# Walking sixteen batches with a loop on the chip instead of straight-line code, in a gated window-attention and router kernel

## The chip, the cores and the metric

The kernel runs on one core of a Trainium2 chip. Its time is device microseconds from start to end of one execution on that core; lower is better. The core has a matrix engine (TensorE, PE in the profile), VectorE (DVE), ScalarE (ACT) and GpSimd (POOL), and a fifth queue, SyncE (SP), which here only issues DMAs. Each of the five has a sequencer of its own that reads its own list of instructions and meets the others only through semaphores.

## The reference

`x` and `ctx` are 16 batches of 256 channels by 2048 positions, float32.

```python
x = x + tanh(g_xattn) * xattn(layernorm(x), ctx)   # layernorm over the 2048 positions
x = x + tanh(g_ffn) * ffn(layernorm(x))

# xattn: 8 heads of 32 channels; position t sees the 16 keys t-8 .. t+7
q, k, v = Wq @ x + bq, Wk @ ctx + bk, Wv @ ctx + bv
attn = softmax(q . k_window * 32**-0.5)
out = Wo @ (attn . v_window) + bo

# ffn: each row of 2048 is routed over 64 experts, the best 8 of the softmax are kept
scores = softmax(flat @ router_weight.T + router_bias)
out = flat * sum(top8) + w_dense @ expert_bias
```

## The kernel before

A batch is cut into four chunks of 512 positions (`NCH`), and the unit of the program is a **step**: chunk `c` of batch `b`, with `par`, which of two buffers the batch uses. A step works on several chunks at once: the scores and softmax of its own chunk (four units, each a half chunk of a 128-channel group), attention and output projection of the chunk before (`attend`, `output`), router columns of the chunk two back (`rows`, `router`), queries of the next chunk, keys and values of the chunk two ahead, and in chunks 2 and 3 the router's result for the batch before (`mixture` on PE, `finish` on DVE).

The order inside a step is written out by hand, once for each engine. On PE it is: `attend(0)`, `queries(1)`, `rows(1)`, `scores(0)`, `attend(1)`, `router`, `scores(1)`, `scores(2)`, mixture, `output(0)` and `output(1)`, `scores(3)`, `values(0)` and `values(1)`, `queries(0)` of the next chunk, `rows(0)`, `keys(0)` and `keys(1)`. A scores unit is one mask matmul of 384 columns and 32 small ones on 32-row tiles; an attend is 51 matmuls of up to 64 columns; a projection (L1099) is 6 matmuls of 512 columns.

DVE takes maxima, shifts, sums and transposes the probabilities (`turn`, L882), and in between it runs three chains of very small operations, each of which waits for the one before by semaphore: the reciprocal roots of the two layer norms (L771 to L783, in chunks 3 and 0) and the router's top 8 (L1023 to L1075, in chunk 1). ACT evicts, takes exponentials and makes the high halves; POOL makes the low halves and the residual sums.

All ordering between operations goes through `need` (L288), a semaphore wait for a count. Semaphores are never set back, so the counts grow with the batch: `nth(b, c, off)` is 4b + c + off + 1, `done(UNITS, ...)` is 16b + something, and others go with 2b, 5b, 8b, 12b, 15b, 64b or 256b. Before the change Python knows every count, and each wait carries a constant. `need` leaves a wait out where the count is zero or less, and `live` and `seq` leave out work beyond the first and the last batch:

```python
        def walk(step):

            for n in range(-2, N + NCH):
                step(n // NCH, n % NCH, (n // NCH) % 2)
```

`N` is 64, so each engine's program is 70 steps of straight-line code with no jump in it.

Of the kernel before, what the change touches and what calls it, by code (L numbers as in the profile page):

```python
# [58 lines left out]
def gated_window_attention_and_router(nc, x, ctx, g_xattn, g_ffn, wqT, bq, wkT, bk, wvT, bv, woT, bo,  # L59
# [11 lines left out]
    with ExitStack() as stack:  # L71
# [200 lines left out]

        def live(b, c, off):

            return 0 <= NCH * b + c + off < N

        def final(b, g, j):

# [4 lines left out]
            return c >= 2 and seq(b - 1)  # L283

        def seq(b):
            return 0 <= b < B

        def need(eng, s, value):  # L288

            if value > 0:  # L290
                eng.wait_ge(s, value)

        def walk(step):

            for n in range(-2, N + NCH):
                step(n // NCH, n % NCH, (n // NCH) % 2)

        def place(c, off):

# [22 lines left out]
        @block.sync  # L322
        def _(sp):

            for i, w in enumerate((wkT, wvT)):
                sp.dma_start(wkv_raw[:, i], w.rearrange("(g p) o -> p g o", g=G)).then_inc(kv_ld, 16)
            for i, v in enumerate((bk, bv)):
                sp.dma_start(bias_kv[:, i], v).then_inc(kv_ld, 16)
            for ch in range(NCH):
                sp.dma_start(x1[0][:, :, cols(ch)],  # L330
                             ctx[0, :, cols(ch)].rearrange("(g p) t -> p g t", g=G)).then_inc(sq0_ld[ch], 16)
            sp.dma_start(wq_raw[:], wqT.rearrange("(g p) o -> p g o", g=G)).then_inc(w_ld, 16)
            sp.dma_start(att[:, :, 0:C], woT.rearrange("(g p) o -> p g o", g=G)).then_inc(w_ld, 16)
            sp.dma_start(bias_q[:], bq).then_inc(w_ld, 16)
            sp.dma_start(bias_o[:], bo).then_inc(w_ld, 16)
            sp.dma_start(gates[:, 0:1], g_xattn.partition_broadcast(P)).then_inc(w_ld, 16)
            sp.dma_start(gates[:, 1:2], g_ffn.partition_broadcast(P)).then_inc(w_ld, 16)
            sp.dma_start(c_in[:], ctx[0, :, cols(0)].rearrange("(g p) t -> p g t", g=G)).then_inc(ctx_in, 16)
            for ch in range(NCH):
                sp.dma_start(x_in[:, :, cols(ch)],  # L340
                             x[0, :, cols(ch)].rearrange("(g p) t -> p g t", g=G)).then_inc(x_ld[ch], 16)
            sp.dma_start(c_sq[:], ctx[1, :, cols(0)].rearrange("(g p) t -> p g t", g=G)).then_inc(sq_ld, 16)
            sp.dma_start(rb[:], rbias.partition_broadcast(P)).then_inc(r_ld, 16)
            sp.dma_start(wr[:], wrT.rearrange("(n p) e -> p n e", p=P)).then_inc(r_ld, 16)
            for half in range(2):
                sp.dma_start(x1[1][half * E:(half + 1) * E, 0, :], experts).then_inc(r_ld, 16)

            sp.wait_ge(sq_rdy, NCH + 1)
            sp.dma_start(c_sq[:], ctx[1, :, cols(1)].rearrange("(g p) t -> p g t", g=G)).then_inc(sq_ld, 16)

            def step(b, c, par):
                if live(b, c, 0):

                    turned, freed = nth(b, c, 0), nth(b, c, -1)
                    for g in range(G):
                        need(sp, vt_rdy[g], turned)
                        need(sp, av_mm[g], freed)
                        for h in range(HPG):
                            sp.dma_start(v_diag[head(h), g, :, head(h)],
                                         v_turn[head(h), g].rearrange("p (j d) -> p j d", d=SUB)).then_inc(vd_ld[g], 16)  # L360
                if live(b, c, 3) and live(b, c, 2):

                    ch, db = place(c, 3)
                    rows_in = ctx[b + db, :, cols(ch)].rearrange("(g p) t -> p g t", g=G)
                    need(sp, cl_rdy, nth(b, c, 2))
                    sp.dma_start(c_in[:], rows_in).then_inc(ctx_in, 16)
                if live(b, c, 8):

                    ch, db = place(c, 8)
                    rows_in = ctx[b + db, :, cols(ch)].rearrange("(g p) t -> p g t", g=G)  # L370
                    need(sp, sq_rdy, nth(b, c, 7))
                    sp.dma_start(c_sq[:], rows_in).then_inc(sq_ld, 16)
                if live(b, c, 0):

                    rows_in = x[b, :, cols(c)].rearrange("(g p) t -> p g t", g=G)
                    for g in range(G):
                        need(sp, x1_rdy[g], nth(b, c, -1))
                    sp.dma_start(x_res[:], rows_in).then_inc(res_in, 16)
                if live(b, c, 5) and live(b, c, 1):

                    ch, db = place(c, 5)
                    rows_in = x[b + db, :, cols(ch)].rearrange("(g p) t -> p g t", g=G)
                    need(sp, xl_rdy, nth(b, c, 1))
                    sp.dma_start(x_in[:, :, cols(ch)], rows_in).then_inc(x_ld[ch], 16)
                if finishing(b, c):

                    g = c - 2
                    rows_out = out[b - 1, g * P:(g + 1) * P, :]
                    need(sp, fin_rdy, final(b - 1, g, NCH - 1))
                    sp.dma_start(rows_out, x1[1 - par][:, g, :]).then_inc(out_st[g], 16)  # L390

            walk(step)
            for g in range(G):
                sp.wait_ge(out_st[g], 16 * (B + 1))
            sp.wait_ge(kv_ld, 16 * 4)
            sp.wait_ge(w_ld, 16 * 6)
            sp.wait_ge(r_ld, 16 * 4)

        @block.gpsimd
        def _(pool):  # L400
# [25 lines left out]
            def step(b, c, par):  # L426
# [87 lines left out]
                    halo(1)  # L514
                if now:
                    low(3)
                if b == -1 and c == 3:
                    experts_split()

            walk(step)  # L520

        @block.scalar
        def _(act):
# [32 lines left out]
            def step(b, c, par):  # L556
# [98 lines left out]
                now, before = live(b, c, 0), live(b, c, -1)  # L655
                if live(b, c, -2):
                    copy_rows(0, -2)
                if live(b, c, 7) and not (b == -1 and c == 2):
                    context_square()
                if live(b, c, 2):  # L660
                    context_high()
# [62 lines left out]
                    keys_high(1, 2)  # L724
                if now:
                    high(3)
                if b == -1 and c == 2:
                    first_queries()
                    context_square()

            walk(step)

        @block.vector
        def _(dve):
# [105 lines left out]
            def step(b, c, par):  # L840
# [54 lines left out]
                    dve.scalar_tensor_tensor(buf[:, g, cols(j)], buf[:, g, cols(j)], row_a[:, g:g + 1],  # L895
                                             ps_a[j % 2][:], ALU.mult, ALU.add).then_inc(fin_rdy, 1)

                if b == 0 and c == 0:

                    dve.wait_ge(sum_mm, 1)  # L900
                    dve.tensor_copy(wr_sum[:], ps_r[:, 0:E]).then_inc(sum_rdy, 1)
                if b == 0 and c == 1:
                    dve.wait_ge(sum_rdy, 2)

                now, before, stats = live(b, c, 0), live(b, c, -1), live(b, c, 4) and live(b, c, 0)
# [99 lines left out]
                if c == 0 and seq(b - 1):  # L1005
# [4 lines left out]
                        dve.bn_aggr(mv_x1[:, g], st_x1[:, g]).then_inc(aggr2, 1)  # L1010
                    need(dve, aggr2, b * (G + 1))
                    inverse_root(root2, (b - 1) * ROOT, mv_x1, var_x1, half_x1, nt_x1, rs_x1, neg_mean_x1, ln2_rdy)
                if b == -1 and c == 2:
                    first_statistics()

            def router_logits(b, stage):
# [58 lines left out]
                    dve.tensor_tensor(wd_cat[:, :, 3 * E + 1:3 * E + 2], wd[:, :, E:E + 1], wd_cat[:, :, 3 * E:3 * E + 1],  # L1075
                                      ALU.subtract).then_inc(wd_rdy, 1)

            walk(step)

        @block.tensor  # L1080
        def _(pe):
# [21 lines left out]
            def step(b, c, par):  # L1103
# [59 lines left out]
                def mixture(j):  # L1163

                    g = c - 2
                    need(pe, wt_rdy, 2 * b)
                    if b == 1:
                        need(pe, ex_rdy, 2)

                    if j < 2 and live(b, c, -1):  # L1170
                        need(pe, ae_rdy[j], nth(b, c, -1))
                    elif j < 2:
                        need(pe, ae_rdy[j], N)
                        need(pe, fin_rdy, final(b - 1, g - 1, 2 + j) if g else 0)
                    else:
                        need(pe, fin_rdy, final(b - 1, g, j - 2))
                    pe.matmul(ps_a[j % 2][:], wd_both[:, g], ex_hi[:, cols(j)], start=True, stop=False)  # L1177
                    pe.matmul(ps_a[j % 2][:], wd_one[:, g], ex_lo[:, cols(j)], start=False, stop=True).then_inc(mix_mm, 1)

                def output(g):  # L1180

                    for i in range(G):
                        need(pe, al_rdy[i], nth(b, c, -1))
                    if b == 0 and c == 1:
                        need(pe, wol_rdy, 1)
                    if live(b, c, 1):
                        need(pe, kh_rdy[g], nth(b, c, 1))
                    project(ps_j[g], wo_hi, wo_lo, g, att_hi, att_lo).then_inc(o_mm[g], 1)

                def router():  # L1190
# [2 lines left out]
                    need(pe, xt_rdy[1], nth(b, c, -2))  # L1193
                    if ch == 0:
                        need(pe, lg_rdy, b * G)
                        if b == 0:
                            need(pe, sum_rdy, 2)
                    for k in range(TB):
                        for g in range(G):
# [80 lines left out]
                if live(b, c, 2):  # L1280
                    keys(0)
                    keys(1)
                if b == -1 and c == 3:

                    pe.wait_ge(r_ld, 16 * 4)
                    for k in range(T // P):
                        ins = pe.matmul(ps_r[:, 0:E], all_ones[:], wr[:, k], start=(k == 0), stop=(k == T // P - 1))
                    ins.then_inc(sum_mm, 1)

            walk(step)  # L1290


# [25 lines left out]
```

## Time and profile before

| | |
|---|---|
| median of 3 runs | 1567.15 us (1563.61 to 1568.27) |
| the profiled execution's own time | 1567.15 us |
| its span, first to last instruction | 1565.0 us |
| mean granted TensorE clock | 0.981 of full speed |
| PE busy | 94% of the span |
| DVE, ACT, POOL busy | 81%, 73%, 73% |

The profiled execution and the median are the same number, and the span is 2.15 us shorter than it. "Idle before" is the time that an engine did nothing ahead of an instruction, with what ended it; a q behind an engine's name (PEq, SPq) means its sequencer. Semaphore waits that stand as instructions of their own have line 291, that of `wait_ge` in `need`, and are not counted as busy.

### The profile page before, as it was taken

What the parts mean: (1) busy time and instruction counts of PE and PEld (TensorE: products, weight loads), DVE (VectorE), ACT (ScalarE), POOL (GpSimd) and SP (SyncE); (2) the same over time, 40 slices, a digit from 0 to 9 for tenths busy, and PEclk for the clock granted to TensorE, in tenths of its full rate; (3) what the DMA queues carried; (4) which work ended last, traced back from release to release, by engine and by line L of the source; (5) the groups of instructions that cost most, each with busy time, mean ns of one, the idle gap of its engine ahead of it and who ended that gap; (6) DMA issues with size and microseconds to landing.
All of it is one profiled execution on the core that took longest, in us unless ns stands there. A gap on an engine that the chain in (4) does not pass through costs nothing.

```text
span 1565.0 us, 66658 instructions
## 1 busy us (share of the span) xinstructions
PE 1469.5 (94%) x28162; PEld 1210.0 (77%) x28162; DVE 1269.8 (81%) x2970; ACT 1148.2 (73%) x2009; POOL 1148.8 (73%) x1110
## 2 busy tenths in 40 slices
PE   2599999999999999999999999999999999999985
PEld 1477887888888888888888887888888788778764
DVE  4377887889888888988888898888889888888864
ACT  3488777778777877877777787777778787767752
POOL 2487877777787878778787777878777787867762
PEclk8799999999999999999999999999999999999997
DMA  6354455554555455455545545554554555434232
GB/s 202 97 143 125 133 138 133 156 150 102 176 139 136 135 157 142 109 177 139 129 139 157 141 111 179 137 131 137 154 146 110 169 144 132 124 85 132 64 73 93
DMA packets 365577, 210.39 MB, mean 134 GB/s; under 512 B 294497, under 2 KB 295521, under 8 KB 361057
## 3 DMA queue, kind: packets, MB, share of 16 engines
q1 hardware_dynamic: 365280, 206.14, 48.6%
q8 instruction: 223, 3.65, 1.0%
q14 instruction: 74, 0.60, 0.1%
HBM read 136.88 MB, written 33.55 MB: 109 GB/s over the span
## 4 chain that ended last, share of the span: by engine, by line
PE 60%; DVE 26%; issue 7%; POOL 2%; ACT 2%; DMA 1%; SPq 1%; POOLq 0%; DVEq 0%; ACTq 0%
PE ps_j L1099 22%; PE ps_a L1123 9%; PE ps_s L1158 9%; PE ps_s L1099 6%; PE ps_r L1200 6%; DVE prob_t L882 3%; DVE wq_lo L805 2%; PE ps_s L1153 2%; DVE p_sum L872 2%; PE ps_t L1140 2%; PE ps_a L1177 2%; DVE lg L1028 2%; DVE neg_max L861 1%; DVE st_x L889 1%; DVE v_turn L853 1%
## 5 line engine op out<-in xcount | busy, mean ns | idle before, releaser
L474 POOL TENSOR_TENSOR score<-score,p_inv 128x384 f32<-128x384 f32 x256 | 221.8, 867 | 117.2 <-DVE p_inv L876 116.1
L481 POOL TENSOR_TENSOR prob<-score,prob 128x384 f16<-128x384 f32 x256 | 266.1, 1040 | 30.8 <-ACT prob L633 30.0
L1158 PEld LDWEIGHTS ps_s<-kv_win,q_col 32*32 32x32 f32 x16384 | 192.9, 105 | 55.2 <-issue 55.2
L1123 PEld LDWEIGHTS ps_a<-prob_t,v_diag 128*128 128x128 f16 x6528 | 198.9, 97 | 42.3 <-DVE prob_t L882 26.2
L1123 PE MATMUL ps_a<-prob_t,v_diag 128*128 128x64 f16 (+1 forms) x6528 | 212.4, 190 | 19.4 <-DVE prob_t L882 16.0
L1158 PE MATMUL ps_s<-kv_win,q_col 32*32 32x48 f32 x16384 | 228.2, 203 | 1.9 <-issue 1.9
L455 POOL TENSOR_TENSOR c_lo<-c_in,c_hi 128x1024 fp32r<-128x1024 f32 x64 | 152.5, 2382 | 98.6 <-ACT c_hi L607 98.6
L882 DVE STREAM_TRANSPOSE prob_t<-prob 128x512 f32<-128x512 f32 x256 | 176.7, 699 | 54.9 <-POOL prob L481 54.9
L1099 PE MATMUL ps_j<-c_hi,wkv_hi 128*128 128x512 f32 x512 | 170.9, 415 | 39.9 <-POOL c_lo L455 29.9
L450 POOL TENSOR_TENSOR att_lo<-att,att_hi 128x512 fp32r<-128x512 f32 x128 | 162.7, 1275 | 60.2 <-ACT att_hi L593 59.4
L571 ACT ACTIVATE kv_win<-ps_j,v_bias 128x512 f16<-128x512 f32 x128 | 106.5, 844 | 109.7 <-PE ps_j L1099 109.7
L872 DVE TENSOR_REDUCE p_sum<-score 128x8 f32<-128x384 f32 x256 | 139.1, 543 | 57.1 <-ACT score L627 54.0
L633 ACT ACTIVATE prob<-score 128x384 f16<-128x384 f32 x256 | 162.6, 635 | 24.9 <-POOL score L474 24.9
L861 DVE TENSOR_REDUCE neg_max<-ps_s 128x8 f32<-128x384 f32 x256 | 139.6, 545 | 49.9 <-PE ps_s L1158 49.0
L461 POOL TENSOR_TENSOR x_lo<-x_in,x_hi 128x1024 fp32r<-128x1024 f32 x64 | 153.9, 2405 | 21.9 <-ACT x_hi L623 21.9
L627 ACT ACTIVATE score<-score 128x384 f32<-128x384 f32 x256 | 130.4, 515 | 50.6 <-DVE score L867 50.5
L469 POOL TENSOR_TENSOR x<-x,x_res 128x512 f32<-128x512 f32 x128 | 163.0, 1294 | 2.7 <-ACT x L652 2.6
L1099 PE MATMUL ps_j<-c_hi,wkv_lo 128*128 128x512 f32 x512 | 160.8, 396 | 0.0
L1099 PE MATMUL ps_j<-c_lo,wkv_hi 128*128 128x512 f32 x512 | 159.6, 393 | 0.0
L867 DVE TENSOR_TENSOR score<-ps_s,neg_max 128x384 f32<-128x384 f32 x256 | 140.3, 548 | 3.9
L846 DVE SCALAR_TENSOR_TENSOR kv_win<-ps_j,v_bias,kv_win 128x512 f16<-128x512 f32 x128 | 98.6, 793 | 54.0 <-ACT kv_win L571 54.0
L563 ACT ACTIVATE kv_win<-ps_j,bkv_col 128x512 f32<-128x512 f32 x128 | 88.2, 689 | 69.4 <-PE ps_j L1099 62.9
(149 smaller groups left out, 3320.6 us busy)
## 6 DMA issues: line engine op xcount, KB each, us to landing
v_diag<-v_turn SPq DMA_DIRECT2D x512, 68.0 KB, 2.8
c_in<-ctx_dram SPq DMA_DIRECT2D x64, 512.0 KB, 4.8
x_in<-x_dram SPq DMA_DIRECT2D x64, 512.0 KB, 5.6
x_res<-x_dram SPq DMA_DIRECT2D x64, 512.0 KB, 4.4
out_dram<-x SPq DMA_DIRECT2D x32, 1024.0 KB, 7.0
c_sq<-ctx_dram SPq DMA_DIRECT2D x60, 512.0 KB, 5.5
x<-ctx_dram SPq DMA_DIRECT2D x4, 512.0 KB, 6.5
x<-experts_dram SPq DMA_DIRECT2D x2, 512.0 KB, 10.9
```

The costliest lines, as they stand in the source:

```text
L450: pool.tensor_tensor(att_lo[:, g], att[:, g], att_hi[:, g], ALU.subtract).then_inc(al_rdy[g], 1)
L461: pool.tensor_tensor(x_lo[:], x_in[:, :, cols(ch)], x_hi[:], ALU.subtract).then_inc(xl_rdy, 1)
L469: pool.tensor_tensor(rows, rows, x_res[:, g], ALU.add).then_inc(x1_rdy[g], 1)
L474: pool.tensor_tensor(score[:, u], score[:, u], p_inv[:, u, :].unsqueeze(2).to_broadcast([P, HALF, KEYS]), ALU.mult).then_inc(pm_rdy, 1)
L481: pool.tensor_tensor(part(prob[:, u % 2], 1)[:, :, 0:KEYS], score[:, u], part(prob[:, u % 2], 0)[:, :, 0:KEYS], ALU.subtract).then_inc(pl_ ...
L633: act.activation(part(prob[:, u % 2], 0)[:, :, 0:KEYS], score[:, u], ACT.Copy).then_inc(ph_rdy, 1)
L861: dve.tensor_reduce(neg_max[:, u], scores_of(u), AX, ALU.max, negate=True).then_inc(mx_rdy, 1)
L872: dve.tensor_reduce(p_sum[:, u], score[:, u], AX, ALU.add).then_inc(su_rdy, 1)
L882: dve.transpose(prob_t[:, u // 2, (u % 2) * CHUNK:(u % 2 + 1) * CHUNK], prob[:, u % 2].rearrange("p n k -> p (n k)")).then_inc(pt_rdy, 1)
L1099: ins = pe.matmul(dst[:], w[:, i, o], v[:, i], start=(n == 0), stop=(n == 2 * G + 1))
L1123: ins = pe.matmul(ps_a[g][:, q0:q1], part(v_diag[:, g, j], kv), part(prob_t[:, g, lo:hi], kp), start=(j == 0 and n == 0), stop=(j == NB), ...
L1158: ins = pe.matmul(s[head(h), n * KEYS:(n + 1) * KEYS], q_col[head(h), g, at:at + SUB], kv_win[c % 2][head(h), 0, g, at:at + KEYS], start=F ...
```

## The change

`walk` is given the engine. The steps of batches -1, 0 and 1 are straight-line code as before, batches 2 to 13 are run by a loop on the chip (`Fori(2, 13, 2)`: six rounds of eight steps, two batches a round so that `par` stays a constant), and batches 14, 15 and 16 (the last for what trails behind) are straight-line code again. Each of the five engines has a loop of its own; nothing joins them at its end.

Inside the loop `b` is a register, not a number. Every semaphore count that has `b` in it, and every address in DRAM that depends on the batch, is then computed by the sequencer of the engine that uses it. On SP two helpers do this ahead of the waits (`count`, `address`); on the other engines `need` hands the expression to `wait_ge`. Tests of the kind `b == 0` are guarded so that they are false in the loop. Which operations run, on what data and in which order is the same, and so are all buffers and semaphores.

```diff
         def live(b, c, off):
-            return 0 <= NCH * b + c + off < N
+            return not isinstance(b, int) or 0 <= NCH * b + c + off < N
...
         def seq(b):
-            return 0 <= b < B
+            return not isinstance(b, int) or 0 <= b < B
 
         def need(eng, s, value):
-            if value > 0:
+            if not isinstance(value, int) or value > 0:
                 eng.wait_ge(s, value)
 
-        def walk(step):
-
-            for n in range(-2, N + NCH):
-                step(n // NCH, n % NCH, (n // NCH) % 2)
+        def walk(eng, step):
+
+            for c in (2, 3):
+                step(-1, c, 1)
+            for b in range(2):
+                for c in range(NCH):
+                    step(b, c, b % 2)
+            with eng.Fori(2, B - 3, 2) as b:
+                for c in range(NCH):
+                    step(b, c, 0)
+                for c in range(NCH):
+                    step(b + 1, c, 1)
+            for b in range(B - 2, B + 1):
+                for c in range(NCH):
+                    step(b, c, b % 2)
...
+            def count(value):
+
+                if not isinstance(value, int):
+                    sp.to_reg(value)
+                return value
+
+            def address(ap):
+
+                if not isinstance(ap.offset, int):
+                    sp.to_reg(ap.offset * 4)
+                return ap
...
-                    turned, freed = nth(b, c, 0), nth(b, c, -1)
+                    turned, freed = count(nth(b, c, 0)), count(nth(b, c, -1))
...
-                    rows_in = x[b, :, cols(c)].rearrange("(g p) t -> p g t", g=G)
+                    rows_in = address(x[b, :, cols(c)].rearrange("(g p) t -> p g t", g=G))
...
-            walk(step)
+            walk(pe, step)
```

## Rows read from the trace of the kernel before

**Rows 1.** The page's head and part 1: busy time by engine.
```profile
span 1565.0 us, 66658 instructions
PE 1469.5 (94%) x28162; PEld 1210.0 (77%) x28162; DVE 1269.8 (81%) x2970; ACT 1148.2 (73%) x2009; POOL 1148.8 (73%) x1110
```

**Rows 2.** Windows: busy us of PE, PEld, DVE, ACT, POOL, then clock, DMA share, GB/s.
```profile
700.00:800.00 100.00, 98.97 (x2036) 82.09 (x2031) 84.71 (x197) 79.51 (x139) 77.19 (x74) 1.00 0.53 145
```

**Rows 3.** The page's part 4, the chain that ended last, by engine.
```profile
PE 60%; DVE 26%; issue 7%; POOL 2%; ACT 2%; DMA 1%; SPq 1%; POOLq 0%; DVEq 0%; ACTq 0%
```

**Rows 4.** Waits: who waited for whom, us in total, times, longest.
```profile
PE ps_a L1123 <- DVE prob_t L882: 16.0, 18, 3.1
PE ps_j L1099 <- DVE kv_win L846: 8.4, 25, 0.6
PE ps_a L1123 <- issue: 2.9, 6, 1.0
```

**Rows 5.** DMA: the instruction queue, and two small loads with time to landing.
```profile
q8 instruction: 223, 3.65, 1.0%
...
wkv_raw<-wkT_dram SPq DMA_DIRECT2D x1, 256.0 KB, 2.8
...
bkv_col<-bk_dram SPq DMA_DIRECT2D x1, 1.0 KB, 2.7
```

**Rows 6.** Timeline from 694.8 to 701.2 us, end of a batch.
```profile
694.80 1.44 DVE L846 SCALAR_TENSOR_TENSOR kv_win<-ps_j,v_bias,kv_win 128x512 f16<-128x512 f32 x2
...
695.60 0.73 PE L1099 MATMUL ps_j<-c_hi,wkv_hi 128*128 128x512 f32 x2 [0.60 <-DVE kv_win L846]
...
698.07 1.25 DVE L889 BATCH_NORM_STATS2 st_x<-x 128x6 f32<-128x512 f32 x2
...
698.46 1.64 PE L1123 MATMUL ps_a<-prob_t,v_diag 128*128 128x32 f16 x51
...
699.25 0.64 ACT L633 ACTIVATE prob<-score 128x384 f16<-128x384 f32 x1
699.51 0.71 DVE L882 STREAM_TRANSPOSE prob_t<-prob 128x512 f32<-128x512 f32 x1 [0.19 <-POOL prob L481]
...
699.74 0.57 ACT L599 ACTIVATE x_t<-ps_t 128x512 f32<-128x512 f32 x1
...
701.15 0.71 DVE L882 STREAM_TRANSPOSE prob_t<-prob 128x512 f32<-128x512 f32 x1 [0.93 <-POOL prob L481]
```

**Rows 7.** Semaphore waits that are instructions of their own, whole span.
```profile
L291 PEldq EVENT_SEMAPHORE  x941: 51/51/1312, 19.3 to 1558.5; - x189
L291 DVEq EVENT_SEMAPHORE  x666: 21/21/21, 14.0 to 1545.5; - x167
```

**Rows 8.** The same on PE, from 711.9 to 712.7 us.
```profile
L291 PEldq EVENT_SEMAPHORE  x4: 51/51/51, 712.2 to 712.5; - x4
```

**Rows 9.** Timeline of PE from 706 to 713 us.
```profile
707.57 0.90 PE L1158 MATMUL ps_s<-kv_win,q_col 32*32 32x48 f32 x64
708.40 0.73 PE L1099 MATMUL ps_j<-att_hi,wo_hi 128*128 128x512 f32 x2
708.97 0.63 PE L1099 MATMUL ps_j<-att_hi,wo_lo 128*128 128x512 f32 x2
709.44 0.62 PE L1099 MATMUL ps_j<-att_lo,wo_hi 128*128 128x512 f32 x2
```

**Rows 10.** Timeline of DVE from 628.9 to 629.9 us, the root of a layer norm.
```profile
629.14 0.16 DVE L779 TENSOR_TENSOR nt_x<-rs_x 128x2 f32<-128x2 f32 x1
629.34 0.16 DVE L781 TENSOR_TENSOR nt_x<-nt_x,half_x 128x2 f32<-128x2 f32 x1
```

**Rows 11.** Waits of SP's own queue, us in total, times, longest.
```profile
SPq L359 <- DVE v_turn L853: 314.3, 64, 14.5
```

**Rows 12.** The line of the router's logits on DVE: ns min/median/max.
```profile
L1028 DVE SCALAR_TENSOR_TENSOR lg<-wd,rs_x,rb x32: 272/1065/1100, 180.7 to 1544.2; 128x64 f32<-128x64 f32 x32
```

**Rows 13.** The small matmuls of the scores: ns min/median/max, first and last start.
```profile
L1158 PE MATMUL ps_s<-kv_win,q_col x16384: 197/201/285, 67.5 to 1520.6; 32*32 32x48 f32 x200
```

More of the change, by code:

```diff
@@ L363, in step @@
                     ch, db = place(c, 3)
-                    rows_in = ctx[b + db, :, cols(ch)].rearrange("(g p) t -> p g t", g=G)
+                    rows_in = address(ctx[b + db, :, cols(ch)].rearrange("(g p) t -> p g t", g=G))
                     need(sp, cl_rdy, nth(b, c, 2))
@@ L369, in step @@
                     ch, db = place(c, 8)
-                    rows_in = ctx[b + db, :, cols(ch)].rearrange("(g p) t -> p g t", g=G)
+                    rows_in = address(ctx[b + db, :, cols(ch)].rearrange("(g p) t -> p g t", g=G))
                     need(sp, sq_rdy, nth(b, c, 7))
@@ L381, in step @@
                     ch, db = place(c, 5)
-                    rows_in = x[b + db, :, cols(ch)].rearrange("(g p) t -> p g t", g=G)
+                    rows_in = address(x[b + db, :, cols(ch)].rearrange("(g p) t -> p g t", g=G))
                     need(sp, xl_rdy, nth(b, c, 1))
@@ L387, in step @@
                     g = c - 2
-                    rows_out = out[b - 1, g * P:(g + 1) * P, :]
+                    rows_out = address(out[b - 1, g * P:(g + 1) * P, :])
                     need(sp, fin_rdy, final(b - 1, g, NCH - 1))
                     sp.dma_start(rows_out, x1[1 - par][:, g, :]).then_inc(out_st[g], 16)
-            walk(step)
+            walk(sp, step)
             for g in range(G):
@@ L516, in step @@
                     low(3)
-                if b == -1 and c == 3:
+                if isinstance(b, int) and b == -1 and c == 3:
                     experts_split()
-            walk(step)
+            walk(pool, step)
         @block.scalar
@@ L657, in step @@
                     copy_rows(0, -2)
-                if live(b, c, 7) and not (b == -1 and c == 2):
+                if live(b, c, 7) and not (isinstance(b, int) and b == -1 and c == 2):
                     context_square()
@@ L726, in step @@
                     high(3)
-                if b == -1 and c == 2:
+                if isinstance(b, int) and b == -1 and c == 2:
                     first_queries()
                     context_square()
-            walk(step)
+            walk(act, step)
         @block.vector
@@ L896, in finish @@
                                              ps_a[j % 2][:], ALU.mult, ALU.add).then_inc(fin_rdy, 1)
-                if b == 0 and c == 0:
+                if isinstance(b, int) and b == 0 and c == 0:
                     dve.wait_ge(sum_mm, 1)
                     dve.tensor_copy(wr_sum[:], ps_r[:, 0:E]).then_inc(sum_rdy, 1)
-                if b == 0 and c == 1:
+                if isinstance(b, int) and b == 0 and c == 1:
                     dve.wait_ge(sum_rdy, 2)
@@ L1012, in step @@
                     inverse_root(root2, (b - 1) * ROOT, mv_x1, var_x1, half_x1, nt_x1, rs_x1, neg_mean_x1, ln2_rdy)
-                if b == -1 and c == 2:
+                if isinstance(b, int) and b == -1 and c == 2:
                     first_statistics()
@@ L1076, in router_weights @@
                                       ALU.subtract).then_inc(wd_rdy, 1)
-            walk(step)
+            walk(dve, step)
         @block.tensor
@@ L1166, in mixture @@
                     need(pe, wt_rdy, 2 * b)
-                    if b == 1:
+                    if isinstance(b, int) and b == 1:
                         need(pe, ex_rdy, 2)
@@ L1183, in output @@
                         need(pe, al_rdy[i], nth(b, c, -1))
-                    if b == 0 and c == 1:
+                    if isinstance(b, int) and b == 0 and c == 1:
                         need(pe, wol_rdy, 1)
@@ L1195, in router @@
                         need(pe, lg_rdy, b * G)
-                        if b == 0:
+                        if isinstance(b, int) and b == 0:
                             need(pe, sum_rdy, 2)
@@ L1282, in step @@
                     keys(1)
-                if b == -1 and c == 3:
+                if isinstance(b, int) and b == -1 and c == 3:
                     pe.wait_ge(r_ld, 16 * 4)
@@ L1288, in step @@
                     ins.then_inc(sum_mm, 1)
-            walk(step)
+            walk(pe, step)
 def kernel(**inputs):
```

## The prediction

> **What bounds the kernel now.** I read the page's head and busy shares first, then the windows, the chain, the waits and last two stretches of the timeline. PE is busy 94% of the span and has 28,162 matmuls with as many weight loads, out of 66,658 instructions in all [rows 1]. The missing 6% lies at the two ends: in a window from the middle PE is busy 98.97 us of 100, at the full granted clock, while DVE is at 84.7 [rows 2]. So there is 1 us in 100 to take back on PE, and whatever holds PE up for longer than that comes out at the end. The chain runs through PE for 60% and through DVE for 26%, with 7% "issue" [rows 3]: DVE is nearly a second bound. PE's own waits are small, 16.0 us for transposed probabilities and 8.4 us, in 25 pieces, for the low half of the values [rows 4]. The schedule is tight in the sense that a late neighbour is felt at once.
>
> The change adds no arithmetic and no data. What it adds is work for the five sequencers, so the questions are what a jump back costs, what a computed count costs, and what lies in front of PE while they happen.
>
> **Part one, five jumps back.** Six rounds make five taken jumps on each engine. The trace of before has no such jump inside the work. What the code list weighs it does show: 223 instruction packets with 3.65 MB [rows 5], 16.4 KB each. A round is two batches of sixteen, so about 28 packets over the five engines, most of them PE's. If the first packet of the body is not at hand when the engine jumps, it must be fetched. The price of a fetch: the queue's 1.0% of 16 engines over 1565 us is 250 us for 223 packets, 1.1 us each, which is the floor; a load of 1 KB lands after 2.7 us and one of 256 KB after 2.8 us [rows 5], and latency and transfer one after the other (2.7 + 1.1) make 3.8 us, the ceiling. I take 2.8 us, the row of a large load.
>
> The Trainium skill says the same from another side ("Runtime: NRT & Kernel Launch", Instruction fetch mechanics): the instruction memory is a window of a few 16 KiB pages filled in sequence, and a taken branch to a page outside it has to wait for a fetch. The 16.4 KB packets agree with its page size; no row here shows the wait. By that page alone POOL and SP, with short bodies, might keep theirs and jump for nothing, which leaves the sum as it is, since it hangs on PE, DVE and ACT.
>
> What covers the 2.8 us? [Rows 6] show the end of a step that ends a batch. PE starts `keys` at 695.60, held by DVE's low halves (the second of them done at 694.80 + 1.44 = 696.24), and the next step's `attend(0)` starts at 698.46. PE's sequencer can pass `keys(1)` only after 696.24, jumps at about 696.5 and has code again at 699.3: PE idles 0.8 us. DVE hands over its last two statistics behind the transpose ahead of 698.07, at about 697.6, and has code at 700.4: the transpose of 699.51 is 0.9 us late, but the one of 701.15, for which PE's second attend waits, is not, because it waits for POOL anyway. ACT is worst off: it hands over its last copy at about 698.7, has code at 701.5, and the copy of 699.74 starts 1.8 us late. Behind it are queued on ACT the square, the context's high half, the queries, the attention's evictions and the first exponential, and DVE waits for that exponential in order, and PE for DVE. The scores' matmuls start from 67.5 to 1520.6 us over 64 steps [rows 13], so a step is 1453.1 / 63 = 23.1 us; ACT is idle for 20% of it [rows 2], 4.7 us, so part is made up. I take 0.8 us on PE and 1.7 us from the neighbours, 2.5 us a jump: 5 x 2.5 = **12.5 us**. Floor: 5 x 1.1 = 5 us with all of it overlapped, or nothing if the fetch is hidden; ceiling: 5 x 3.8 = 19 us plus as much as a second late packet, 25 us. Entering and leaving the loop is straight ahead and costs one such gap at most; it is inside these ends.
>
> **Part two, counts in registers.** The loop holds 12 batches, 48 steps. In each, PE's `need` calls use some 40 waits, but many counts recur: in order of the code I count about eight new values a step on PE (four of the 16b kind, one for the next chunk, one of 256b, and in chunks 2 and 3 those of `fin_rdy`), if a value once made is kept. The trace shows no register instruction of that kind. The nearest rows are the stand-alone waits: 51 ns on PE and 21 on DVE [rows 7]; back to back on PE, four of them lie between 712.2 and 712.5 [rows 8], so 0.1 us apart. I take 0.1 us for each new value on PE.
>
> Where does it lie behind other work? Ahead of and inside the projections PE has 0.24 us of array work for each weight load and matmul (twelve from 695.60 to 698.46) [rows 6], and the sequencer runs ahead. Not so after the small matmuls of a scores unit: 64 records in the 0.83 us from 707.57 to 708.40, and the next projection then takes 0.57 us to its second pair against 0.47 later on (708.40, 708.97, 709.44) [rows 9]; its waits already show as 0.1 us of gap. A step has four such seams (after `scores(0)`, `(1)`, `(2)` and `(3)`), and by my count three fresh values fall on or just behind them: the two units' counts of `sh_rdy` and the next chunk's. That is 3 x 0.1 = 0.3 us a step, 48 x 0.3 = **14.4 us**. The other values lie beneath projections, which costs nothing while those stand; without that cover the remaining five would be 0.5 us a step.
>
> DVE's small chains get a new value for every link. A link is 0.16 us long and starts 0.2 us after the one before [rows 10], and the value for the next wait can be made while it runs, so I put them at nothing; at DVE's 21 ns a piece uncovered, some 40 links a batch would be 40 x 12 x 0.021 = 10 us. ACT and POOL are idle for 20% and 23% [rows 2]. SP waits 314 us for DVE alone [rows 11] and its sums are made before its waits, so that the loads leave a few tenths later at most, into buffers that are not waited for. Floor of the part: nothing. Ceiling: all eight values exposed and half as many waits more standing alone, 12 x 0.1 = 1.2 us a step, 58 us.
>
> **The sum**, against the profiled execution's own 1567.15 us, which is also the median: 1567.15 + 12.5 + 14.4 = **1594 us**, 1.7% slower.
>
> **The rivals.**
>
> *Only the jumps.* Register values are made ahead of time everywhere, because PE's sequencer is faster with them than with a wait (a wait's record is 51 ns, not 100). For it: PE is kept busy 99 of 100 us with 941 stand-alone waits already on it [rows 7]. Then 1567.15 + 12.5 = 1580 us.
>
> *The counts are the larger cost.* A wait for a register's value rides on no matmul, so it stands alone and behind each scores unit there are several gaps of 0.1 us. For it: the seam of [rows 9]. Against: nothing in this trace has such a wait. 1567.15 + 58 + 12.5 = 1638 us.
>
> *No change that can be measured.* The code of the body's start is there when the jump comes, or is fetched under PE's 2.9 us of `keys`, and the rest is hidden. "Issue" holds PE for only 2.9 us in six pieces ahead of the attends, though the code is fetched all along [rows 4], so fetching in sequence costs nothing. 1567 us.
>
> *Faster.* One mechanism: DVE's logits take 272 ns at best but 1065 at the median [rows 12], so something on the core, most likely POOL's work beside it, holds DVE. The 32 of them lose 32 x 0.79 = 25 us, on the chain, 19 of it in the loop. If the sequencers' delays shift POOL's long operations off that place, half of it, 9 us, comes back: 1558 us. It decides only if the jumps cost under 1.8 us each and the counts nothing. Nothing makes POOL move the right way, so it is unlikely.
>
> **How the numbers follow.** Chances: forecast 0.50, only the jumps 0.18, counts larger 0.15, no change 0.12, faster 0.05. A difference below 0.3%, 4.7 us, is about what a measurement of this kernel can't tell from no change. All of the first three lie above that: slower 0.83, same 0.12, faster 0.05. The likeliest case's own range is 1580 to 1612 us. The range to hold 8 in 10 leaves out faster and half of no change below (0.11) and the upper half of the counts' case above (0.07): 1569 to 1638 us.
>
> **What the changed profile would show.** PE's idle time put down to "issue" grows from almost nothing, with five long pieces about 185 us apart, near the ends of batches 3, 5, 7, 9 and 11, each 1 to 4 us, and such a piece on DVE and ACT at the same places; the steps inside a round are 23.4 us and not 23.1. Busy time of every engine and the number of matmuls stay as they are, and so does the granted clock. Batches 0, 1, 14 and 15 take what they took. The prediction is wrong in its first part if no such piece is there, or if it is over 5 us; in its second if the 48 steps inside the loop are as long as before, or over 1 us longer each, and I would then look at the seams behind the scores and at DVE's chains.

## The result, and the profile after

The changed kernel takes 1618.67 us (1618.11 to 1618.87, 4 runs) against 1567.23 us: 1.033 times, 95% interval 1.031 to 1.035. It is slower by 51.4 us; 27 were forecast, inside a range that reached to 1638.

The page's head, part 1, the instruction queue of part 3 and the first line of part 4 of the changed kernel:

```profile
span 1616.3 us, 68923 instructions
...
PE 1485.2 (92%) x28162; PEld 1220.9 (76%) x28162; DVE 1271.2 (79%) x2970; ACT 1148.2 (71%) x2009; POOL 1147.7 (71%) x1110
...
q8 instruction: 234, 3.83, 1.0%
...
PE 51%; DVE 19%; issue 13%; POOL 11%; ACT 3%; DMA 2%; SPq 1%; DVEq 0%; POOLq 0%; ACTq 0%
```

Beside [rows 1, 3], the engines have the same operations and DVE, ACT and POOL are busy for the same time; "issue" has gone from 7% to 13% of the chain. PE is busy 16 us longer with the same matmuls, so some of them ran slower. The waits say where "issue" lies (who waited for whom, us in total, times, longest):

```profile
PE ps_a L1146 <- issue: 30.5, 12, 5.3
DVE prob_t L905 <- issue: 26.4, 5, 5.4
ACT x_t L622 <- issue: 22.8, 5, 4.7
```

Before the change the first of these was 2.9 us with 1.0 at the longest [rows 4]. Five waits of about 5 us on each of three engines are the five returns. The timeline at the second one, which answers to [rows 6]:

```profile
624.72 2.74 PE L1146 MATMUL ps_a<-prob_t,v_diag 128*128 128x32 f16 x51 [5.32 <-issue]
625.30 0.60 ACT L622 ACTIVATE x_t<-ps_t 128x512 f32<-128x512 f32 x1 [4.67 <-issue]
625.51 1.30 DVE L905 STREAM_TRANSPOSE prob_t<-prob 128x512 f32<-128x512 f32 x2 [5.41 <-issue]
...
627.30 1.20 PE L1122 MATMUL ps_s<-x_hi,wq_hi 128*128 128x512 f32 x2
```

The loop's own instructions have line 300, and the counts made in registers line 291 (count, ns min/median/max, first and last start):

```profile
L300 PEldq COMPARE_BRANCH  x6: 83/6930/7091, 424.5 to 1386.1; - x6
...
L300 DVEq COMPARE_BRANCH  x6: 55/63/63, 425.7 to 1387.3; - x6
```

```profile
L291 DVEq ALU_OP  x540: 40/40/52, 242.9 to 1383.6; - x180
L291 PEldq ALU_OP  x420: 32/32/42, 239.9 to 1381.7; - x140
```

PE's five taken jumps last 7 us each, the sixth, which falls through, 0.083. DVE's record of a jump is short, but its next operation comes as late. Not every engine stands still. `FUSED_REGOPS` on line 300 is the first instruction of the next round, and at the second return it comes 0.3 us after the jump on SP and POOL, 5.6 on ACT, 6.9 on DVE and 7.1 on PE, and at the other four returns the same within 0.3 (ns of the record, then its start in us):

```profile
L300 SPq COMPARE_BRANCH  x1: 45/45/45, 618.2 to 618.2; - x1
...
L300 SPq FUSED_REGOPS  x1: 50/50/50, 618.5 to 618.5; - x1
...
L300 ACTq COMPARE_BRANCH  x1: 45/45/45, 619.6 to 619.6; - x1
...
L300 POOLq COMPARE_BRANCH  x1: 45/45/45, 620.7 to 620.7; - x1
L300 POOLq FUSED_REGOPS  x1: 50/50/50, 621.0 to 621.0; - x1
...
L300 ACTq FUSED_REGOPS  x1: 50/50/50, 625.1 to 625.1; - x1
```

A round has 191 records on SP, 214 on POOL, 489 on ACT, 598 on DVE and 7200 on PE, so it is the two short bodies that go on at once, as the prediction had thought possible. The windows around the return on PE (us from and to, length, busy and count of PE, PEld, DVE, ACT, POOL, granted clock, DMA share, GB/s):

```profile
619.40:624.70 5.30, 0.00 (x0) 0.00 (x0) 0.70 (x2) 1.21 (x2) 2.31 (x5) 0.78 0.82 315
624.70:629.60 4.90, 4.88 (x57) 4.41 (x58) 2.59 (x4) 2.58 (x4) 1.64 (x1) 0.54 0.07 18
629.60:632.00 2.40, 2.40 (x99) 2.03 (x98) 0.72 (x2) 2.05 (x4) 0.73 (x1) 1.00 0.01 3
```

While PE stands still its granted clock goes to the lower level, 1.2 GHz, and it stays there for most of the next 4.9 us: the 51 matmuls of `attend(0)` take 2.74 us, where before they took 1.64 [rows 6]. From `attend(0)` to the first scores it takes 5.61 us (624.72 to 630.33), where before it took 3.66 (698.46 to 702.12).

There is a third thing, that no step of the prediction has. In the first step of the second batch of a round, PE stops in the middle of a run of small matmuls that wait for nothing:

```profile
341.85 0.79 PE L1181 MATMUL ps_s<-kv_win,q_col 32*32 32x48 f32 x54
343.81 0.35 PE L1181 MATMUL ps_s<-kv_win,q_col 32*32 32x48 f32 x10 [1.17 <-issue]
```

For the account I take the length of each step, from the start of its first small scores matmul to that of the next step's. Of the span's 51.3 us, 47.5 lie between the start of batch 2 and that of batch 14 (1148.07 against 1100.53). 40.6 are five steps of chunk 3 that grew by 8.8, 7.3, 7.4, 9.1 and 8.0, the returns; 6.7 are the six chunk 0 of the odd batches (0.4 to 1.6 each); 0.3 is all the other 37 steps together. The other 3.8 us are in the warm-up and from batch 14 on (1.5 and 2.3 us), where single executions differ by as much; chunk 0 of batch 14, the step behind the loop, is 2.1 us longer and the next one 2.6 shorter.

### The profile page after: what moved, and what is told of

The parts are those of the page before. It is cut to its first block, busy times and chain, and to the rows that moved or that the text cites. A ratio compares the mean times of both kernels' runs of the same rounds, so it can differ in the third digit from the quotient of the medians.

```text
span 1616.3 us, 68923 instructions
## 1 busy us (share of the span) xinstructions
PE 1485.2 (92%) x28162; PEld 1220.9 (76%) x28162; DVE 1271.2 (79%) x2970; ACT 1148.2 (71%) x2009; POOL 1147.7 (71%) x1110
## 4 chain that ended last, share of the span: by engine, by line
PE 51%; DVE 19%; issue 13%; POOL 11%; ACT 3%; DMA 2%; SPq 1%; DVEq 0%; POOLq 0%; ACTq 0%
PE ps_j L1122 18%; PE ps_a L1146 8%; PE ps_s L1181 7%; PE ps_s L1122 6%; PE ps_r L1223 4%; DVE prob_t L905 2%; POOL x L492 2%; POOL score L497 2%; POOL att_lo L473 2%; PE ps_a L1200 2%; POOL x_lo L484 2%; PE ps_t L1163 2%; PE ps_s L1176 1%; PE ps_a L1201 1%; POOL c_lo L478 1%
## 5 line engine op out<-in xcount | busy, mean ns | idle before, releaser
L1146 PE MATMUL ps_a<-prob_t,v_diag 128*128 128x64 f16 (+1 forms) x6528 | 218.5, 193 | 46.0 <-issue 30.5
L1146 PEld LDWEIGHTS ps_a<-prob_t,v_diag 128*128 128x128 f16 x6528 | 205.6, 99 | 70.5 <-issue 48.0
L1122 PEld LDWEIGHTS ps_j<-c_hi,wkv_hi 128*128 128x128 f32 x512 | 89.5, 191 | 67.3 <-POOL c_lo L478 25.2
```

Source lines behind the costliest of these rows:

```text
L1122: ins = pe.matmul(dst[:], w[:, i, o], v[:, i], start=(n == 0), stop=(n == 2 * G + 1))
L1146: ins = pe.matmul(ps_a[g][:, q0:q1], part(v_diag[:, g, j], kv), part(prob_t[:, g, lo:hi], kp), start=(j == 0 and n == 0), stop=(j == NB), ...
```

## The experiments

All are built on the two kernels; times are medians, each with its ratio to the kernel before on the same chip.

**No return, one return.** The loop body is ten batches and runs once, or six and runs twice.

```diff
-            with eng.Fori(2, B - 3, 2) as b:
-                for c in range(NCH):
-                    step(b, c, 0)
-                for c in range(NCH):
-                    step(b + 1, c, 1)
-            for b in range(B - 2, B + 1):
+            with eng.Fori(2, 4, 10) as b:            # one return: Fori(2, B - 7, 6), range(6)
+                for k in range(10):
+                    for c in range(NCH):
+                        step(b + k, c, k % 2)
+            for b in range(12, B + 1):               # one return: as it was
```

> The loop has one round of ten batches (2 to 11), so counts and addresses come from registers in 40 steps, but no engine ever jumps back. Theory J (the loss is that of the five returns, 8 us each): 1567 to 1571 us. Rival C (computed counts cost most of it, about 1 us a step): 40/48 of the 51 us, 1605 to 1612 us.

> Two rounds of six batches: one return in place of five, registers in the same 48 steps. J: 1567 + 8 for the return, and up to 6 for the late packets of about 1.2 us that the changed kernel shows once a round, 1575 to 1583 us. C: unchanged at 1610 to 1619 us.

1582.07 us (1.0088, 1.0052 to 1.0124) without a return; 1590.67 us (1.0137, 1.0094 to 1.0181) with one. Both theories missed the first: J by 11 us, C by 23. The lengths of its steps say why. Chunks 1, 2 and 3 of batches 2 to 13 are 22.30, 23.60 and 24.34 us on average, against 22.33, 23.61 and 24.32 before; chunk 0 is 22.56 against 21.45. Whatever costs time there sits in chunk 0 alone, though every step makes its counts in registers. With one return, that one step is 31.68 us, 7.4 longer, and chunk 0 is long again, which is why J missed this kernel too, by 8 us (C by 19).

**The jump named ahead.**

```diff
-            with eng.Fori(2, B - 3, 2) as b:
+            with nc.Fori(2, B - 3, 2, engines=[eng.engine], hint_back_edge=True) as b:
```

> The changed kernel with one instruction more at the head of each round on each engine, which names the jump to come so that its target can be fetched ahead. If the cost of a return is the fetch of the first packet (J): PE's idle pieces of 5.3 us shrink below 1 us and the time is 1568 to 1582 us. If it is the jump itself or the emptied queue (rival K): still 1610 to 1619 us.

1609.12 us (1.025, 1.0201 to 1.0299): 9.5 us back, not 37 to 51. Yet the long stops are gone. The source view of line 300 in this kernel:

```profile
L300 PEldq BRANCH_PREFETCH_HINT  x6: 36/36/45, 236.7 to 1175.8; - x6
...
L300 PEldq COMPARE_BRANCH  x6: 88/357/419, 422.5 to 1364.8; - x6
```

A taken jump lasts 0.36 us instead of 7, and DVE and ACT too are at the next round within 0.6 us, so it was the fetch. Chunk 3 before a return grows by 1.0 us on average, not 8.1, but chunk 0 behind it is 2.5 to 3.0 us longer, which it was not without the hint. The rest stands as stops of about 1 us inside runs of small matmuls, two of them behind the return at 612 us. In the timeline of PE and its waits:

```profile
615.91 0.27 PE L1181 MATMUL ps_s<-kv_win,q_col 32*32 32x48 f32 x3
617.29 0.87 PE L1181 MATMUL ps_s<-kv_win,q_col 32*32 32x48 f32 x61 [1.12 <-issue]
...
622.74 0.87 PE L1181 MATMUL ps_s<-kv_win,q_col 32*32 32x48 f32 x61
624.64 0.27 PE L1181 MATMUL ps_s<-kv_win,q_col 32*32 32x48 f32 x3 [1.04 <-issue]
```

```profile
PE ps_s L1181 <- issue: 20.9, 21, 1.5
```

Where the loop ended there was a stop of 3.2 us more, and two steps there, chunk 3 of batch 13 and chunk 1 of batch 14, were 10 us longer together.

**Who has to loop.** PE's code a loop and the other four straight, or the other way about.

```diff
+            if eng.engine != PE_ENGINE:     # the other kernel: ==
+                for b in range(2, B - 2):
+                    for c in range(NCH):
+                        step(b, c, b % 2)
+            else:
+                with eng.Fori(2, B - 3, 2) as b:
+                    ...
```

> Only TensorE's code is a loop with five returns; the other four engines run straight-line code with constants. Theory P (PE's own stop is the cost, the neighbours' lie under it): 5.3 us idle and about 2 us for the half clock behind it, 5 x 7.3 = 36 us, so 1600 to 1612 us, or more if everything is PE's. Rival N (the neighbours' lateness, as I had it for two thirds of a return): PE's part is small, 1575 to 1590 us.

> TensorE runs straight-line code with constants; the other four engines loop, with five returns and computed counts. If their stops and counts lie wholly under TensorE's in the changed kernel but would cost on their own (DVE's transposes were 5 us late behind a return): 5 x 4 = 20 us, 1583 to 1592 us. If they cost nothing even on their own: 1563 to 1570 us.

PE alone: 1613.94 us (1.0285, 1.0241 to 1.033), nearly the whole loss. The other four alone: 1595.30 us (1.0184, 1.0152 to 1.0216), more than half of it; each is 2 to 3 us above what I expected. In the traces the chunk 3 steps at the returns grow by 7.8 to 9.1 us with PE alone, and by 3.8 to 4.7 with the others alone, where 0.9 to 2.3 more come in the chunk 0 behind. So the two are not a sum: the engines stop at the same time. With the others looping, PE reaches `rows(1)` and waits for ACT, which has been standing for 4.5 us:

```profile
617.48 0.60 ACT L628 ACTIVATE x_t<-ps_t 128x512 f32<-128x512 f32 x1 [4.50 <-issue]
...
618.22 1.08 PE L1169 MATMUL ps_t<-ident,x 128*128 128x128 f32 x4 [3.54 <-ACT x_t L628]
```

**The place of the code.** The PE records of the kernel before are 2 x 28,162 [rows 1] and 941 waits [rows 7], 57,265; the instruction queue q8 moved 223 packets [rows 5]. That is 257 records a packet: q8 carries PE's code alone, 256 instructions in a packet. (The 9,387 records of the other engines go with queue q14, 74 packets and 0.60 MB: like q8's 3.65 MB, 64 bytes a record.) So I counted PE's records up to the first small matmul of each chunk 0, modulo 256, the place. In the kernel before a batch is 3575 records, 9 less than 14 packets, and the place creeps from 181 in batch 2 to 64 in batch 15. Idle matmuls, four records each, put into the warm-up shift it:

```diff
+                if isinstance(b, int) and b == -1 and c == 2:
+                    for _ in range(16):      # 32 for 128 places, 40 for 160, 62 for 248
+                        pe.matmul(ps_r[:, 0:2], all_ones[:], w_sq[:, 0:2], start=True, stop=True)
```

> The kernel before with 16 idle matmuls (64 TensorE instructions) in the warm-up, where TensorE waits for 24 us: every later instruction sits 64 places further in its packet of 256. Theory A (chunk 0 of a batch loses 0.9 to 1.6 us wherever a packet's edge falls in its run of small matmuls, and the kernel before happens to miss that): some chunk 0 steps grow from 21.3 to 22 or 23 us, time 1568 to 1580 us. Rival R (the loss in chunk 0 comes from the register instructions): 1563 to 1569 us.

> The same with 32 idle matmuls, 128 places. A: other batches than with 64 places have the long chunk 0, time 1568 to 1585 us. R: 1563 to 1569 us.

> The kernel with ten batches of register counts and no return, with the same 128 places put in. A: the loss of 1.2 us in ten chunk 0 steps changes with the place, in part or in all of them; time anywhere from 1567 to 1582 us but not the 1582 of the unshifted one in the same steps. R: the ten chunk 0 steps stay 1 to 1.5 us longer, 1579 to 1585 us.

1579.85 us (1.0099, 1.0062 to 1.0136) and 1583.19 us (1.0089, 1.0057 to 1.012) for straight-line code with constants, no loop and no register in it; 1576.82 us (1.0065, 1.0043 to 1.0087) for ten batches of register counts with 128 places. The last can't be told by its time from the same kernel without the shift (1.0088), so for it only the steps speak. The length of chunk 0 with its place, from the traces:

```
                         batch:    2      4      6      8     10     12     14
before                   place   181    163    145    127    109     91     73
                            us  22.86  21.31  21.31  21.31  21.39  21.31  21.84
64 places                place   245    227    209    191    173    155    137
                            us  22.09  21.97  22.57  22.52  21.33  21.31  21.31
128 places               place    53     35     17    255    237    219    201
                            us  21.73  22.84  22.24  22.33  22.67  22.61  22.64
registers, no return     place   186    215    243     15     43     70     52
                            us  23.04  23.01  22.26  22.33  22.90  22.03  21.69
registers, 128 places    place    58     87    115    143    171    198    180
                            us  28.15  21.31  21.31  21.31  21.31  22.61  21.73
```

Over batches 2 to 15 of these five and of the one with 248 places below, all 36 steps whose place is from 80 to 175 are short (21.51 us at most), and 46 of the 48 others are longer than 21.55, at the median 22.3. Register counts don't matter to it. The stops themselves say it more directly. In these six kernels PE stood for more than 0.25 us with nothing to wait for 76 times from batch 2 on, for 0.6 us at the median and 1.95 at most, and each time the record that came next had number 193 to 195, modulo 256. A shift moves the work, and the stops stay at the same number. (Of the odd batches, which the table leaves out, two are much longer than the rest, 25.96 us in batch 5 with 128 places and 26.31 in batch 3 with registers and 128.) In the timeline of PE with 128 places, a stop at such a place, in code with no register:

```profile
429.93 0.58 PE L1123 MATMUL ps_a<-prob_t,v_diag 128*128 128x32 f16 x14
431.87 1.23 PE L1123 MATMUL ps_a<-prob_t,v_diag 128*128 128x64 f16 x37 [1.36 <-issue]
```

The Trainium skill ("Runtime: NRT & Kernel Launch", Instruction fetch mechanics) says that crossing a 16 KiB boundary is mostly hidden in sequential code, because instructions are dispatched more slowly than they are fetched. "Mostly" holds here: of some 220 crossings in the kernel before, 12 show a stop of over 0.25 us. For those in or just behind a run of small matmuls the measurement differs, up to 1.95 us on PE, and the measurement decides.

**Both together.**

> Two rounds of six batches as in the kernel with one return, and 40 idle matmuls (160 TensorE places) in the warm-up, so that all twelve chunk 0 steps of the loop lie where a shift had cost nothing. If the return (8 us) and the packets' edges (about 1.1 us in each of eleven steps) add up: 1590.7 - 12 = 1577 to 1581 us. If computed counts cost something of their own, or the places are not what matters: 1585 us or more.

> The changed kernel with the same 160 places. Its five returns stay, the six chunk 0 steps of the odd batches lose their 0.4 to 1.6 us (6.7 us in all): 1610 to 1613 us. If the places are not what matters: 1618 us.

> Hint and 160 places together. The hinted kernel lost 3.9 us at each of five returns, about 1.1 in each chunk 0 of an odd batch and about 11 where the loop ends. With the places right, the chunk 0 losses go (5.5 us) and the part of a return that lies in chunk 0 of the next batch (2.7 of the 3.9 us) goes if it is a packet's edge: 1590 to 1597 us. If that part belongs to the return: 1602 to 1605 us.

> The kernel before with 62 idle matmuls (248 places, so 8 back from where it was). Its one long chunk 0 (batch 2, 22.9 us) should come to 21.3, the last batch keeps its own: 1564 to 1567 us, at best 2 us faster than before, which may not be told from no change. If it is slower by 3 us or more, the idle matmuls or the places cost something that I have not understood.

With 160 places the chunk 0 steps of the loop lie in the free stretch.

| kernel | without shift | with shift |
|---|---|---|
| one return | 1590.67 | 1572.14 (1.0036, 1.0016 to 1.0057) |
| the changed kernel, five returns | 1618.67 | 1601.79 (1.0213, 1.0179 to 1.0247) |
| five returns, named ahead | 1609.12 | 1577.96 (1.0068, 1.0045 to 1.009) |
| kernel before (248 places) | 1567.23 | 1567.03 (1.000, 0.998 to 1.002) |

The kernels of one row ran on different chips, and the kernel before took 1565.86 to 1567.95 us on them. The three loops gain, and 5 to 12 us more than I expected: with the hint it is mostly the 10 us at the loop's end, which I hadn't expected to go, and for the other two I have no account. In the changed kernel the six odd chunk 0 are back at 21.3 to 21.4 us, and the five returns are 7.1 to 8.1 us now instead of 7.3 to 9.1. In the one with one return, batches 2 to 13 take 1106.5 us, 5.9 more than before, with a return of 7.5 us in them: 48 steps of register counts cost nothing at all. Its seam behind a scores unit is the same as in [rows 9]: 0.58 us to the second pair, then 0.47:

```profile
706.63 0.74 PE L1121 MATMUL ps_j<-att_hi,wo_hi 128*128 128x512 f32 x2
707.21 0.63 PE L1121 MATMUL ps_j<-att_hi,wo_lo 128*128 128x512 f32 x2
707.68 0.62 PE L1121 MATMUL ps_j<-att_lo,wo_hi 128*128 128x512 f32 x2
```

With hint and shift a return hardly shows in the loop. Batches 2 to 13 take 1101.8 us, 1.2 us more than in the kernel before, with five returns in them. After the jump at 606.4 us PE goes on at once and has one stop of 0.65 us left:

```profile
608.47 1.64 PE L1146 MATMUL ps_a<-prob_t,v_diag 128*128 128x32 f16 x51
...
613.52 0.36 PE L1181 MATMUL ps_s<-kv_win,q_col 32*32 32x48 f32 x13 [0.65 <-issue]
```

Of the 10 us in the two steps at the loop's end 1.0 is left. Yet the whole kernel is slower than the one before, clear of noise, and of the 11 us between the two spans (1576.0 and 1565.0) 10 lie outside the loop: 3.1 in the warm-up and 6.7 from batch 14 on. One thing there is seen in both hinted kernels and in no other trace of this case: DVE stands for 2.4 or 2.5 us behind the loop, in the chain of a layer norm, and PE then waits 5.1 us for DVE's transpose instead of 2.4.

```profile
1369.00 1.81 DVE L794 TENSOR_SCALAR var_x<-mv_x 128x2 f32<-128x2 f32 x1 [2.46 <-issue]
```

It may be the price of the last hint, which names a jump that isn't taken; no run tests that.

No version beats the kernel before: its places are nearly the best by luck. Moving them by 248 brings its long batch 2 from 22.86 to 21.31 us, as expected, and changes nothing in the time that can be measured.

## Why the prediction was right or wrong

**The bound.** Right: PE holds the time, and what stops PE for longer than the 1 us in 100 comes out at the end. The others' operations took as long as before.

**Part one, the returns.** Right in kind, 12.5 us forecast, 40.6 us measured. The step that failed is the price of the fetch, 2.8 us from the landing of a large load. The jump takes 7 us on PE, beyond my ceiling of 3.8, and the next operations of DVE and ACT come 5 us late. That no cover is left then costs the half clock as well: 1.95 us on PE in the timeline above. At the second return 5.32 + 1.95 = 7.3 us, which is what that step grew by. That the fetch is the cost, and not the jump, is shown by the hinted kernels (7 us against 0.36). The Trainium skill's rule ("Runtime: NRT & Kernel Launch", Instruction fetch mechanics) that a taken branch out of the window waits for a fetch agrees with the trace: PE, DVE and ACT stood, and POOL and SP with their short bodies went on after 0.3 us; how long it takes stands only in the trace.

My split of a return, 0.8 us for PE and 1.7 for the neighbours, was wrong in form: each side alone costs more than half of it, and together they overlap. I also read the 223 packets as the code of five engines; they are PE's alone.

**Part two, register counts.** 14.4 us forecast, nothing measured. The count was nearly right (420 `ALU_OP` records on line 291 on PE in 48 steps, 8.8 a step, and 54 `FUSED_REGOPS`, against my eight), and so was the place of the seams. The step that failed is that they lie on the path: their records are 32 ns, below the 0.1 us I took from the waits, and behind a scores unit the gap is 0.11 us with them and 0.10 without. Of the values the prediction put under other work, on DVE's chains too, none showed.

**What was missing.** 6.7 us of stops at packet edges in the six chunk 0 of the odd batches. They come with the change only in that it moves the code: in straight-line code the same stops appear when it is moved by 64 or 128 places. The prediction dismissed this in a rival ("fetching in sequence costs nothing"), from a kernel whose places happened to miss it in all batches of the loop but batch 2.

**The rivals.** "Only the jumps" is the nearest in kind, at three times its price. "Counts are the larger cost" ended near the measured time for a wrong reason: 1638 us was its price, and the kernel with one return and 160 places loses nothing in its loop but the return. Its mechanism, more waits that stand alone, went the other way: on PE they fell from 941 [rows 7] to 749. "No change" failed because the code was not there at the jump, and "Faster" did not come about. So the direction and the range held, and the middle was off by half: one term was three times too small (28 us short), one was not there at all (14 us too much, which made up for half of that), and a third was absent. That the range held is luck. Its upper part came from the counts, which cost nothing; the likeliest case's own range ended at 1612 us, and the jumps alone at their ceiling of 25 us would have ended at 1592.

**Signs named.** Five long pieces near the ends of batches 3 to 11: there, at 5.0 to 5.3 us, above the 1 to 4 named and over the 5 that the prediction gave as a sign of being wrong in its first part. Steps at 23.4 us throughout: not so, which was the sign for the second part; only chunk 3 at a return and odd chunk 0 changed. Clock unchanged: wrong, the mean fell from 0.981 to 0.970.

**Open.** Why chunk 0 alone shows the packet edges, and why batch 1 never does (21.3 to 21.4 us at places 63, 183, 191 and 255), was not tested; that the other chunks follow DVE and have slack on PE is only argued. Nor is it known why chunk 0 of the even batches behind a return takes 21.4 to 21.5 us in the changed kernel, when the same code took 22.2 in the first round. The shifted kernels spread by 6 to 14 us from one execution to the next and the kernel before by 8 to 13, the changed one by 1, and I have no cause for that; the step lengths are those of one execution each. How much the half clock costs was read, not isolated. Why PE's fetch takes 7 us, when its packet occupies a DMA engine for 1.1, stays open.

## What to carry to other kernels

A loop on the chip costs by its returns, not by its register arithmetic: here 8 us for each, with PE, DVE and ACT standing at once, as long as the first packet of the body has to be fetched at the jump, and next to nothing once it is named ahead and the places are right. With the jump named and the places as they were, a return still cost 3.7 us and the loop's end 10. Make rounds long, name the jump, and only then look at counts. A difference of 1% between two programs with the same work may be nothing but where the code falls in its packets: shift one of them by some idle instructions before a cause is believed.

## What the runs showed of the hardware that was not expected

A taken jump to code that was not at hand held TensorE's sequencer for 6.8 to 7.1 us in the changed kernel, and up to 7.4 in the others. On POOL and SyncE, whose rounds are 214 and 191 records, the same jump cost 0.3 us. TensorE's code comes in packets of 256 instructions, and at some packets' edges in or just behind a run of small matmuls (64 weight loads and as many matmuls in 0.81 us) it stood for up to 1.95 us, in straight-line code too. A stop of 5 us, and one of 1.95 us in the shifted register kernel (chunk 0 of 28.15 us), is followed by a stretch at the lower clock (0.54 and 0.50). A register addition took 32 ns on TensorE and 40 on VectorE and was hidden wherever it stood.
